# Rotary step of a batched attention kernel: the swapped halves are read straight out of PSUM by VectorE

## The reference

```
def _rotate_half(x):
    x1, x2 = jnp.split(x, 2, axis=-1)
    return jnp.concatenate([-x2, x1], axis=-1)
q = (x @ wq).reshape(B, T, H, HD).transpose(0, 2, 1, 3)
k = (x @ wk).reshape(B, T, KV, HD).transpose(0, 2, 1, 3)
q = q * cos + _rotate_half(q) * sin
k = k * cos + _rotate_half(k) * sin
scores = jnp.einsum('bhtd,bhsd->bhts', q, k) * (1.0 / np.sqrt(HD))
```

## Time and profile before

| | |
|---|---|
| time, median of 3 runs | 572.55 us (570.56 to 573.87) |
| span of the profiled execution | 571.9 us |
| PE busy | 536.6 us (94%) |
| DVE busy | 423.0 us (74%) |
| ACT busy | 299.0 us (52%) |
| POOL busy | 278.4 us (49%) |
| mean granted TensorE clock | 0.969 |
| stages, first projection to last scores | about 59 to 502 us of the span |

### The profile page before, as it was taken

One profiled execution on the slowest core, in us unless ns is written; L12 is line 12 of the kernel. 1 busy time (PEld: TensorE's weight loads), 2 busy tenths in 40 slices (PEclk: granted clock), 3 DMA queues, 4 the chain that ended last, 5 costly groups with the idle time before them and its releaser, 6 DMA issues.

```text
span 571.9 us, 8828 instructions
## 1 busy us (share of the span) xinstructions
PE 536.6 (94%) x2987; PEld 432.6 (76%) x2988; DVE 423.0 (74%) x600; ACT 299.0 (52%) x504; POOL 278.4 (49%) x204
## 2 busy tenths in 40 slices
PE   4999999999999999999999999999999999899690
PEld 2987888888788878887888888878887888688420
DVE  5647366877697769776978697869777867776786
ACT  2503317563756475647564756475557555543724
POOL 6418314833684268327832774277427743720002
PEclk8899999999999999999999999999999999989866
DMA  7441300110111011101110220012002000000003
GB/s 250 161 148 43 123 2 1 42 52 1 47 55 66 0 56 51 58 0 65 53 47 0 73 68 24 0 73 84 7 0 73 6 0 1 0 2 1 1 0 147
DMA packets 18046, 26.87 MB, mean 47 GB/s; under 512 B 1995, under 2 KB 6219, under 8 KB 18028
## 3 DMA queue, kind: packets, MB, share of 16 engines
q1 hardware_dynamic: 18028, 26.63, 13.4%
HBM read 24.53 MB, written 2.10 MB: 47 GB/s over the span
## 4 chain that ended last, share of the span: by engine, by line
PE 67%; DVE 16%; issue 7%; ACT 7%; POOL 1%; DMA 1%; SPq 0%; DVEq 0%; ACTq 0%; POOLq 0%
PE bank L585 19%; PE bank L587 18%; PE bank L586 18%; PE bank L648 3%; PE bank L649 3%; PE bank L763 2%; DVE s_nat L855 2%; PE bank L633 2%; ACT p_st L433 1%; DVE s_nat L863 1%; PE bank L577 1%; DVE p_tr L868 1%; DVE s_sum L859 1%; DVE s_nat L849 1%; DVE s_nat L851 1%
## 5 line engine op out<-in xcount | busy, mean ns | idle before, releaser
L838 DVE TENSOR_TENSOR q_swap<-q_swap,cst 128x512 f32<-128x512 f32 x80 | 75.5, 944 | 68.5 <-ACT q_swap L404 68.4
L300 POOL TENSOR_TENSOR q_rot<-q_cos,q_swap 128x512 f32<-128x512 f32 x64 | 82.4, 1293 | 55.7 <-DVE q_cos L839 55.7
L585 PE MATMUL bank<-hT_hi,wq_hi 128*128 128x512 f32 x256 | 101.3, 396 | 4.4 <-DVE q_cos L839 4.4
L585 PE MATMUL bank<-wo_hi,o_hi 128*128 128x512 f32 x256 | 102.3, 400 | 0.4 <-issue 0.4
L587 PE MATMUL bank<-wo_hi,o_lo 128*128 128x512 f32 x256 | 100.9, 394 | 0.0
L586 PE MATMUL bank<-wo_lo,o_hi 128*128 128x512 f32 x256 | 100.5, 393 | 0.0
L587 PE MATMUL bank<-hT_hi,wq_lo 128*128 128x512 f32 x256 | 100.0, 391 | 0.0
L586 PE MATMUL bank<-hT_lo,wq_hi 128*128 128x512 f32 x256 | 100.0, 391 | 0.0
L403 ACT ACTIVATE q_swap<-bank 64x512 f32<-64x512 f32 x80 | 47.7, 596 | 63.1 <-POOL k_rot L300 24.6
L287 POOL TENSOR_TENSOR v_lo<-v_all,v_st 64x512 fp32r<-64x512 f32 x32 | 47.6, 1487 | 67.4 <-ACT v_st L414 64.6
L442 ACT ACTIVATE o_hi<-bank 128x512 fp32r<-128x512 f32 x64 | 38.1, 597 | 60.5 <-PE bank L649 60.1
(11 more groups left out here) (148 smaller groups left out, 947.9 us busy)
## 6 DMA issues: line engine op xcount, KB each, us to landing
raw_q<-in_L_attn_wq SPq DMA_DIRECT2D x8, 1024.0 KB, 5.5
raw_o<-in_L_attn_wo SPq DMA_DIRECT2D x8, 1024.0 KB, 5.3
xacc<-in_x SPq DMA_DIRECT2D x4, 512.0 KB, 8.4
raw_k<-in_L_attn_wk SPq DMA_DIRECT2D x8, 256.0 KB, 2.8
out<-xacc SPq DMA_DIRECT2D x8, 256.0 KB, 2.0
raw_o<-in_L_attn_wv SPq DMA_DIRECT2D x1, 1024.0 KB, 7.2
raw_q<-in_L_attn_wv SPq DMA_DIRECT2D x1, 1024.0 KB, 6.9
q_rot<-in_L_ffn_qweight SPq DMA_DIRECT2D x1, 1024.0 KB
```

Of the source, the lines that this page charges most:

```text
L300: pool.tensor_tensor(dst, q_cos[b][:], q_swap[b][:], ALU.add).then_inc(rope_done, 1)
L585: pe.matmul(dst, l_hi, r_hi, start=(i == 0), stop=False)
L838: dve.tensor_tensor(by_t(q_swap[b][:]), by_t(q_swap[b][:]), sin_b, ALU.mult)
```

## The change

ACT's `swap` goes away, with its semaphore. DVE now waits for the projection itself and does three multiplications: the whole bank by the cosine, then the bank's upper 64 partitions by the sine of those partitions into the lower 64 of `q_swap`, and the bank's lower 64 by theirs into the upper 64. The sign of the sine table is turned round, since the sine is now taken at the partition that is read and not at the one that is written. The semaphores `rope_done` and `rope_mul` and the buffers stay as they are.

```
-    sign = np.where(np.arange(HD) < HD // 2, -1.0, 1.0).astype(np.float32)
+    sign = np.where(np.arange(HD) < HD // 2, 1.0, -1.0).astype(np.float32)
...
-            def swap(g, r, k):
-                n = 2 * ITEMS * g + ITEMS * r + k
-                b = (ITEMS * r + k) % 2
-                act.wait_ge(proj_mm, n + 1)
-                if not (isinstance(g, int) and 2 * g + r == 0 and k < 2):
-                    act.wait_ge(rope_done, n - 1)
-                ps = q_ps[ITEM_BANK[k]]
-                act.activation(q_swap[b][0:P // 2, :], ps[P // 2:P, :], ACT.Copy)
-                act.activation(q_swap[b][P // 2:P, :], ps[0:P // 2, :], ACT.Copy).then_inc(swap_done, 1)
...
                 if split_wo is not None:
                     wo_high(split_wo, range(0, 2))
-                swap(*cur, 0)
                 if split_wo is not None:
                     wo_high(split_wo, range(2, 4))
-                swap(*cur, 1)
-                swap(*cur, 2)
                 if last is not None:
                     o_high(*last, 0)
-                swap(*cur, 3)
                 if last is not None:
                     o_high(*last, 1)
-                swap(*cur, 4)
...
             def rope(g, r, k):
                 n = 2 * ITEMS * g + ITEMS * r + k
                 b = (ITEMS * r + k) % 2
-                dve.wait_ge(swap_done, n + 1)
+                dve.wait_ge(proj_mm, n + 1)
                 if not (isinstance(g, int) and 2 * g + r == 0 and k < 2):
                     dve.wait_ge(rope_done, n - 1)
-                dve.tensor_tensor(by_t(q_swap[b][:]), by_t(q_swap[b][:]), sin_b, ALU.mult)
-                dve.tensor_tensor(by_t(q_cos[b][:]), by_t(q_ps[ITEM_BANK[k]][:]), cos_b,
-                                  ALU.mult).then_inc(rope_mul, 1)
+                ps = q_ps[ITEM_BANK[k]]
+                low, high = slice(0, P // 2), slice(P // 2, P)
+                dve.tensor_tensor(by_t(q_cos[b][:]), by_t(ps[:]), cos_b, ALU.mult)
+                dve.tensor_tensor(by_t(q_swap[b][low]), by_t(ps[high]), sin_b[high], ALU.mult)
+                dve.tensor_tensor(by_t(q_swap[b][high]), by_t(ps[low]), sin_b[low], ALU.mult).then_inc(rope_mul, 1)
```

More of the change, by code:

```diff
@@ L148, in build @@
         qk_hi_done, qk_lo_done, wo_hi_done, wo_lo_done = (sem(n) for n in ("qk_hi_done", "qk_lo_done", "wo_hi_done", "wo_lo_done"))
-        proj_mm, swap_done, rope_mul, rope_done = sem("proj_mm"), sem("swap_done"), sem("rope_mul"), sem("rope_done")
+        proj_mm, rope_mul, rope_done = sem("proj_mm"), sem("rope_mul"), sem("rope_done")
         scores_mm, soft_step, exp_done = sem("scores_mm"), sem("soft_step"), sem("exp_done")
```

## The result

The changed kernel takes 562.6 us in the median of four runs (562.34 to 563.0) against 571.55 for the kernel before; the ratio is 0.9855, with a 95% interval from 0.9816 to 0.9894. Faster by 9 us where 6.6 were forecast. The profiled execution has a span of 560.5 us where the one before had 571.9.

The account below looks back on a forecast made before the run. PE was taken as the bound, with ACT or DVE work counting only through PE's waits. 6.6 - 2.8 + 2.8 = 6.6 us less brought the span from 571.9 to 565.3, the median to 565.9 us; range 562.0 to 573.5.

Parts of the forecast that it names:

- The bound and the mechanism: PE busy 94% bounds the kernel; its `r = 1` item 3 waits come from DVE waiting 1.53 us for ACT's copies.
- The gain in `r = 1`: Item 3's wait for the rotary step goes away in all eight `r = 1` stages: 6.6 us gained.
- The price of a step: DVE's three products per item: two halves at 0.71 us each plus 0.68, so 2.10 us.
- The shorter bound of 1.90: Other bound for DVE's three products per item, if they overlap: 0.61 + 0.61 + 0.68 = 1.90 us.
- The loss in `r = 0`: PE starts item 3 0.40 us later in each of seven `r = 0` stages: 2.8 us lost.
- The last stage: Scores 2.2 us sooner and no clock drop behind them, 1.6 us back: 3.8 together, 2.8 added to the sum.
- my rounding down: Last stage's added gain taken as 2.8 instead of 3.0 us, because POOL's stretching of `p_low` might differ.
- the likeliest case: Whole kernel, the terms as summed: a time between 562.5 and 569.5 us, chance 0.5.
- The 0.65 us between span and median: Whole kernel: the median of the runs lies 0.65 us above the profiled span, added to reach 565.9 us.
- the first: Rival: no new wait in `r = 0`, by a 1.90 step or gentler collisions; 9.4 us less, 563.2; chance 0.15.
- the third: Rival: clock still drops in last stage, collisions add 0.4 us per `r = 0` stage; 2 us less, 570.5; chance 0.2.
- The losing side: Second rival: DVE bounds each stage's start, first rope step 1.2 us later than forecast; 7 us more, 580; chance 0.12.

Follow-up runs that it names:

- the aligned products: Changed kernel with three products on all 128 partitions, none moving partitions, so the halves are not exchanged: 560.25 us, ratio 0.9832.
- three products, copies kept: Kernel before with the change's three products out of PSUM, ACT's copies and DVE's wait for them kept: 578.53 us, ratio 1.0101.
- with ScalarE kept busy: Changed kernel with ACT copying unchanging data of the old size into spare tiles, at the old places with the old waits: 562.26 us, ratio 0.9867.
- fourth product: Changed kernel with the first half product of each item done twice, the extra one into a spare tile: 576.14 us, ratio 1.0076.
- copies first: Kernel before with ACT's copies of item 0 moved ahead of the first two `wo_high`: 568.04 us, ratio 0.9933.
- the rope ahead of `p_low`: Changed kernel with the next stage's item 0 rope ahead of `p_low` on DVE, before both kinds of stages: 580.51 us, ratio 1.0157.

## Why the prediction was right, and where its terms were off

**The bound and the mechanism** held. DVE waited for copies that stood behind `p_high` and `wo_high` on ACT; moving them alone gives 4.7 us in the fourteen stages (0, 1) to (7, 0), the whole change 5.1, and keeping them where they are, with the new products, loses.

**The gain in `r = 1`**: 6.6 us forecast over eight stages, of which 5.8 fall on the seven in the table; 5.8 measured. The eight waits were not alike, as I had taken them: 0.83 us in three stages, where the product of L855 in front had been stretched to 1.85 us, 0.36 in three where it took 0.69, and 0.16 and 0.67 at the ends. To spare, I said 0.4 us. It was 0.9 in stages (1, 1), (2, 1), (4, 1) and (6, 1), in front of which that product now takes 0.69, and 0.4 in (3, 1) and (5, 1), where it takes 1.85.

**The price of a step**: 2.10 us forecast with starts 0.71 apart, 2.10 measured in (3, 0) (228.75 to 230.85). The shorter bound of 1.90 is what the aligned products show, 1.20 + 0.68 = 1.88.

**The loss in `r = 0`** is the term that was mis-sized: 2.8 us forecast, 0.7 measured. The step costs what I said. What moved is the end of `p_low` in front of it: 13.04 us behind the scores' start in (2, 1) before, 12.65 after, so 0.39 of the 0.40 us is given back; over the seven stages 0.16 to 0.41 each, 2.1 us in all, and 2.8 less 2.1 is the 0.7 measured. It comes from the softmax products with two inputs in SBUF, the mask above all (1.64 before, 1.41 after). In front of (4, 0) and (6, 0) the mask still took 1.63, and those are the two stages that went to 28.17. The mask product starts a little behind one of POOL's `qk_lo`, and in all seven stages of both kernels it ends 0.58 to 0.62 us behind the start of the next, wherever it had started: it stands still until POOL's instruction is through. I had written that these collisions would "fall out differently" and left their sum as it was. Their size follows the phase of POOL's `qk_lo` against the scores. Over the runs, in stage (2, 1):

| kernel | first `qk_lo`, from the scores of (2, 1) | mask product |
|---|---|---|
| before | -0.63 us | 1.64 us |
| three products, copies kept | -0.54 | 1.71 |
| changed, and with ScalarE kept busy | -2.1 | 1.41, 1.42 |
| fourth product | -0.09 | 1.10 |
| copies first | -0.20 | 0.80 |

It is a matter of where between two starts of POOL's, 1.25 us apart, the product falls, and no steady trend. POOL gets to `qk_lo` behind its last add; the rope steps set that time, not ACT. I had a time for the last add (216.1, 1.6 us ahead of the scores) and didn't carry it into the softmax. It would have had to be better than that: the add ended 2.1 us ahead, and by the table 0.43 us of phase (-0.63 to -0.20) takes 0.84 us off the mask product, twice what was at stake in a stage.

**The last stage**: 3.6 us forecast (0.8 among the eight and 2.8 added), 2.37 + 1.55 = 3.9 measured. The scores came 2.4 us sooner where I said 2.2, PE's wait is 1.3 where I said 1.4, and the clock stays up behind it. In the changed kernel, the stretch and the chain that answer to the earlier trace rows:

```profile
494.00:496.00 2.00, 2.00 (x9) 1.68 (x10) 1.91 (x3) 0.00 (x0) 0.00 (x0) 1.00 0.03 8
```
```profile
492.88 1.08 PE bank L617 x32
...
496.93 0.69 DVE xacc L880
...
505.67 0.38 PE bank L632
```

`accumulate` is 4.05 us behind the scores here and was 5.65 before. `p_low` of this stage was stretched as before (4.39 us against 4.42), so my rounding down had no object.

**The number**: 562.6 us is 0.6 us inside the fast end of the range and 3.3 under the forecast, at the very edge of what I had called the likeliest case. The sum was 2.5 us short, 2.1 of it the loss in `r = 0`; that the phase of `qk_lo` fell out kindly is luck, since I had not worked it out. The 0.65 us between span and median were no property of the kernel either. In every later run the time is 1.8 to 1.9 us above its own span, by which a span of 571.9 belongs to some 573.7 us, the slow end of the kernel before.

**The rivals**: the first (no new wait in `r = 0`, 563.2 us) came closest in number, and its reason was the right one in part: gentler collisions, not a shorter step; the waits are shorter, not gone. Of the third nothing came: the clock stayed up, and the collisions gave time back instead of costing more. The losing side, DVE as the bound, needs a delay that the change doesn't have, but it is nearer than I thought: the fourth product puts it there, since rope steps add up to the scores. The Trainium skill's rule on held instructions ("VectorE: DVE Perf Modes", section "Two Vector instructions with no wait between them") is borne out in both directions, 0.60 to 0.62 us between products that start at the same partitions and 0.69 to 0.72 between others. Another section of that page, "The TRN2 errata — SBUF-src ops pay a fixed extra latency per instruction", gives a Vector instruction a larger fixed part out of PSUM than out of SBUF; these rows don't show it, since products out of PSUM take 0.68 to 0.69 us and undisturbed ones out of SBUF the same.

## What to carry to other kernels

An engine with half its time idle can still set the pace through its order: look at what the copy stands behind on that engine before paying for doing without it (moving one line gave 4 of the 9 us). When work goes to a busier engine, count the steps that lie in a row up to the next consumer, here five up to the scores, and not the one that waits first. And when the order changes, work out anew which of POOL's instructions now run beside DVE's products out of SBUF: that was worth 2 us in one place and went with a loss of 18 in another.

## What the runs showed of the hardware

- DVE products that start on other partitions than their predecessor's follow it after 0.69 to 0.72 us instead of 0.60 to 0.62; the number of partitions (32, 64, 128) leaves the duration at 0.68 to 0.69 us.
- A DVE instruction with both inputs in SBUF beside POOL's subtractions took up to 1.85 us instead of 0.68 (four in a row 6.90 instead of 2.83), and POOL's took up to 1.83 instead of 1.29. With one input in PSUM none of the changed kernel's 240 products took more than 0.695 us. That agrees with the Trainium skill ("SBUF — State Buffer", section "Who interferes with whom"), by which a Vector instruction with two SBUF inputs contends with a GpSimd instruction that reads SBUF, and one with at most one SBUF input does not.
- In the last stage the granted clock fell from the 2.4 GHz level to the 1.2 GHz level behind an idle stretch of PE of 2.6 to 3.6 us (five runs), not behind one of 0.7 to 1.3 us (six runs); with ten filler matmuls in the 2.7 us it stayed up. No length of one wait settles it, though: with the rope ahead of `p_low` it fell once behind waits of 1.04 and 0.74 us close together, and not in four other stages with the same two.
